# Attention of the second block: second score products two steps behind the first, exponentials ahead of the maxima's transfer

## The chip, the cores and the metric

One Trainium2 chip, one of its cores. The metric is the time of one execution in device microseconds (us), the median over several. The engines: TensorE (PE, matrix products), VectorE (DVE), ScalarE (ACT), GpSimd (POOL) and SyncE (SP), which only issues DMAs. ACT can issue DMAs from a queue of its own.

## What is computed

Two transformer blocks, one behind the other, on x of 8 × 512 × 256 (8 items, 512 tokens, 256 features; 16 heads of 16). Cut to what matters here, the second block:

```python
qkv = (x @ qkv_w).reshape(b, n, 3, H, D)
scores = jnp.einsum('bhnd,bhmd->bhnm', q, k) * scale
scores = jnp.where(mask, scores, -jnp.inf)      # mask: the keys of 384 to 511 that are padding
attn = jax.nn.softmax(scores, axis=-1)
out = jnp.einsum('bhnm,bhmd->bhnd', attn, v)
attn_out = out.transpose(0, 2, 1, 3).reshape(b, n, c) @ proj_w + proj_b
x = x + gate_msa[:, None, :] * _modulate(_layernorm(attn_out), shift_msa, scale_msa)
mlp_out = jax.nn.gelu(x @ fc1_w + fc1_b, approximate=False) @ fc2_w + fc2_b
x = x + gate_mlp[:, None, :] * _modulate(_layernorm(mlp_out), shift_mlp, scale_mlp)
```

The mask that the second block gets is the logical not of the valid positions, so only keys among the last 128 count. The kernel reads from the data that this is so and then takes a short form of the attention, with 128 keys a head; it has the general form beside it.

## The kernel before

The work goes item by item: turn n attends item n (n = 0 to 7 of the first block, n = 8 to 15 of the second) and carries along the dense work of the items beside it: for item n − 1 the turning of the attention rows ("t3"), the output product ("wout"), the turning for the MLP ("t2"), its first layer ("up") and second layer ("down"), and for item n + 1 the turning of the input ("t1") and its queries and keys ("qk"). The order on each engine is written out by hand. In the short form (`short(n)`, the second block) a turn is a loop over steps p; each step has three places k = 3p, 3p + 1, 3p + 2 at which the table `HEADS` names dense pieces, and `HEADS_DOWN` says which chunks of the second layer TensorE does there. There are 32 chunks, eight for each of the four token tiles: one product of 128 × 256 in f32, which stands as two rows in TensorE's order of the trace. The walks over `HEADS` are made by every engine, so a piece that is moved in the table moves on TensorE, ACT and VectorE alike.

Heads go in pairs q = 0 to 7. What happens to one pair:

- `pair_scores_of` (L919): four products give the scores of all 512 queries against 128 keys for both heads, in the two `score` banks. It waits for `peaks_ready` of the pair before, since that read the same bank.
- `peaks_of` on VectorE: the maximum over keys (L1432), split into a high and a low part (L1437, L1439).
- `turn_peaks` (L926): TensorE turns these into rows, in the first `score` bank.
- `take_peaks` on VectorE (L1447): the negated rows go into `peaks`, of which there is one. It waits for `peaks_loaded` of the pair before.
- `load_peaks` on ACT (L1131): a DMA on ACT's queue puts `peaks` (8 KB) into four rows of `q_rows`.
- `turned_scores_of` (L938): the second score products, keys on the partitions, with those four rows as further terms, so that the maximum is already subtracted. It waits for `peaks_loaded` of its pair and for the exponentials that free its `turned` bank.
- `head_exp` on ACT (L1125): the exponentials, two a pair.

For two pairs (four heads) there follow `attend_heads` (L948, value products), `take_heads_out` on ACT (L1145), `heads_to_tokens` (L956) and `divide_heads` on VectorE (L1455, L1457). The turn's t3 waits for the last of these.

Beside that SP loads for the next turn, in its own order: the stores of the queries and keys of item n + 1, the store of the output, the residual and modulation rows (L352, L355), then with `load_few(n + 1, g)` the query and key rows of the four groups g of four heads, each behind a `turned_ready` that says that group g's second score products of this turn are done.

ACT holds either the exponential's or the GELU's function table; `ACT_TABLE_LOAD` changes it.

Of the kernel before, what the change touches and what calls it, by code (L numbers as in the profile page):

```python
# [18 lines left out]
def build(nc, d, out):  # L19
    B, L, D = d["x"].shape  # L20
    H = d["L0_cond_torus_scale"].shape[0]
# [47 lines left out]

    HEADS = {0: [("v", 3), ("t3", 0), ("t3", 1)], 1: [("t1", 0), ("t1", 1)], 2: [("wout", 0), ("wout", 1)],
# [3 lines left out]
             19: [("down", 0)], 23: [("down", 1)], 28: [("down", 2)], 35: [("down", 3)]}  # L76
    HEAD_STEPS = H // 2 + 4
    HEADS_DOWN = {16: (0, 6), 19: (6, 10), 20: (10, 11), 22: (11, 14), 23: (14, 16), 25: (16, 20), 26: (20, 21),
                  28: (21, 24), 29: (24, 25), 31: (25, 28), 34: (28, 29), 35: (29, 32)}

    ANY = {0: [("v", 0), ("v", 1)], 1: [("t3", 0), ("t3", 1)], 2: [("v", 2), ("v", 3)], 3: [("t1", 0), ("t1", 1)],
           4: [("wout", 0)], 5: [("wout", 1)], 6: [("wout", 2)], 7: [("wout", 3)], 9: [("qk", 0)],
# [32 lines left out]
    PLACE = []  # L115
    for second in (HEADS, ANY):
        order = listed(FIRST, -1)
# [12 lines left out]
    with ExitStack() as ctx:  # L130
# [134 lines left out]
        def short(n):  # L265
            return n >= B and not chosen["any"]
# [506 lines left out]
        def _(pe):  # L773
# [215 lines left out]
            def turn(n):  # L989
                if short(n):  # L990
                    for p in range(HEAD_STEPS):
                        attended = p >= 5 and p % 2 == 1
                        if 2 <= p < 2 + H // 2:
                            pair_scores_of(n, p - 2)
                        for k in range(3 * p, 3 * p + 2):
                            for piece, m in pieces(HEADS, k, n):
                                dense(piece, m)
                            if k in HEADS_DOWN:
                                down_chunks(n - 1, *HEADS_DOWN[k])
                        if attended:  # L1000
                            attend_heads(n, (p - 5) // 2)
                        if 3 <= p < 3 + H // 2:
                            turned_scores_of(n, p - 3)
                        if 2 <= p < 2 + H // 2:
                            turn_peaks(n, p - 2)
                        for piece, m in pieces(HEADS, 3 * p + 2, n):
                            dense(piece, m)
                        if 3 * p + 2 in HEADS_DOWN:
                            down_chunks(n - 1, *HEADS_DOWN[3 * p + 2])
                        if attended:  # L1010
                            heads_to_tokens(n, (p - 5) // 2)
                    return
                table, down = (FIRST, FIRST_DOWN) if n < B else (ANY, ANY_DOWN)
                for k in range(STEPS):
                    if k < UNITS and not begun(n, k) and not (n < B and amid(n, k - 1)):
                        scores(n, k)
                    if n + 1 < B and k in AHEAD:
                        scores(n + 1, AHEAD[k])
                    if k >= ATTEND and (k - ATTEND) % 4 == 0 and (k - ATTEND) // 4 < GQ:
                        attend(n, (k - ATTEND) // 4)  # L1020
                    if TURN <= k < TURN + UNITS:
                        turn_unit(n, k - TURN)
                    if k >= TOKENS and (k - TOKENS) % 4 == 0:
                        to_tokens(n, (k - TOKENS) // 4)
                    for i, (piece, m) in enumerate(pieces(table, k, n)):
                        if n < B and amid(n, k) and i == 2:
                            scores(n, k + 1)
                        dense(piece, m)
                    if n > 0 and k in down:
                        down_chunks(n - 1, *down[k])  # L1030
                for gq in range(GQ):
                    if TOKENS + 4 * gq >= STEPS:
                        to_tokens(n, gq)
# [9 lines left out]
        def _(act):  # L1043
# [120 lines left out]
            def turn(n):  # L1164
                if short(n):
                    for p in range(HEAD_STEPS):
                        for k in range(3 * p, 3 * p + 2):
                            for piece, m in pieces(HEADS, k, n):
                                dense(piece, m)
                        if p == 0 and n - 2 >= B:  # L1170
                            normalize(n - 2)
                        if p >= 5 and p % 2 == 1:
                            take_heads_out(n, (p - 5) // 2)
                        if 2 <= p < 2 + H // 2:
                            load_peaks(n, p - 2)
                        if 3 <= p < 3 + H // 2:
                            for a in range(2):
                                head_exp(n, 2 * (p - 3) + a)
                        for piece, m in pieces(HEADS, 3 * p + 2, n):
                            dense(piece, m)  # L1180
                        if n == B and p == 6:
                            take_high(w_out, raw_out[1], "wout_loaded", "out_high", 2)
                        if n == B and p == HEAD_STEPS - 1:
                            take_high(w_up, raw_up[1], "wup_loaded", "up_high", 2)
                    return
                for k in range(STEPS):
                    if k >= OUT and (k - OUT) % 4 == 0:
                        take_out(n, (k - OUT) // 4)
                    for piece, m in pieces(FIRST if n < B else ANY, k, n):
                        dense(piece, m)  # L1190
                    if 1 <= k <= UNITS:
                        exps(n, k - 1)
                    if n < B and k + 2 < UNITS and bias_by_act(k + 2):
                        make_bias(n, k + 2)
                    if n == B - 1 and k in (6, 7):
                        take_qkv_high(k - 6)
                    if n == B and k == 15:
                        piece_ready(act, ("wout", TT - 1), n - 1)
                        take_high(w_out, raw_out[1], "wout_loaded", "out_high", 2)
                for gq in range(GQ):  # L1200
                    if OUT + 4 * gq >= STEPS:
                        take_out(n, gq)
                if n == B:
                    take_high(w_up, raw_up[1], "wup_loaded", "up_high", 2)
# [10 lines left out]
        def _(dve):  # L1215
# [293 lines left out]
            def turn(n):  # L1509
                if short(n):  # L1510
                    for p in range(HEAD_STEPS):
# [15 lines left out]
                            dense(piece, m)  # L1527
                        if p == 1 and n == B:
                            first_norm("stats", 1, n - 1)
                        if p >= 5 and p % 2 == 1:  # L1530
                            divide_heads(n, (p - 5) // 2)
                        if n == B and p == 6:
                            take_low(w_out, raw_out[1], "out_high", "out_split", 2)
                    if n == B:
# [84 lines left out]
```

## Time and profile before

| | |
|---|---|
| time, median of 3 runs | 1422.58 us (1421.8 to 1427.55) |
| the profiled execution: time, span | 1422.82 us, 1421.0 us |
| TensorE busy | 1298.0 us, 91% |
| VectorE, ACT, GpSimd busy | 798.7, 765.3, 755.1 us |
| mean granted TensorE clock | 0.982 |

In the rows below, a time at a row's start is in us from the start of the span, then comes the duration of the row (rows of equal instructions in a row are merged, with their count behind the x), and in brackets how long the engine sat idle before it and what it then waited for. "issue" in such a bracket means that the trace shows nothing that it waited for. Busy times of TensorE are modelled: products are pipelined, so the start of one to the start of the next is the better measure.

### The profile page before, as it was taken

The page shows a single profiled execution, that of the slowest core. Times are in us where ns is not written, and L with a number is a line of the kernel's source. Part 1 is how long each engine was busy: PE and PEld are TensorE (multiplying, and loading weights), DVE is VectorE, ACT ScalarE, POOL GpSimd, SP SyncE. Part 2 cuts the span into 40 slices and gives each one's busy share as a digit, 9 for nine tenths or more (in the row PEclk, how much of TensorE's full clock was granted, in tenths as well). Part 3 has the DMA queues.
Part 4 walks back from the last instruction along what each step waited for, and adds up shares of the span by engine and source line. Part 5 has one row for each costly group of instructions (what it writes and reads, how often), then busy time and mean ns, then how long its engine had stood idle before and what let it go on. Part 6 is the DMA issues. An engine that isn't in the chain of part 4 may idle for free. (4 is left out here: it accounts for less than half of the span.)

```text
span 1421.0 us, 24552 instructions
## 1 busy us (share of the span) xinstructions
PE 1298.0 (91%) x8789; PEld 994.6 (70%) x8789; DVE 798.7 (56%) x2240; ACT 765.3 (54%) x1262; POOL 755.1 (53%) x939
## 2 busy tenths in 40 slices
PE   4899999999999999999999996989888888888887
PEld 3577777777787788777787785666666666565656
DVE  3766746746646646647646544464564646464452
ACT  3466665765765765756755753454535444454432
POOL 3698867867877777777777751021322224041323
PEclk9899999999999999999999998999999999999988
DMA  8432322322323313213314316363425243332100
GB/s 259 138 117 56 87 86 53 98 75 67 99 60 84 94 49 90 91 44 91 100 36 111 112 25 185 99 181 87 163 58 163 78 138 101 114 130 74 46 2 30
DMA packets 98259, 133.98 MB, mean 94 GB/s; under 512 B 16802, under 2 KB 51498, under 8 KB 98130
## 3 DMA queue, kind: packets, MB, share of 16 engines
q1 hardware_dynamic: 96850, 131.80, 31.8%
q8 instruction: 73, 1.20, 0.4%
q10 hardware_dynamic: 1280, 0.53, 0.1%
q14 instruction: 56, 0.46, 0.1%
HBM read 72.64 MB, written 58.75 MB: 92 GB/s over the span
## 5 line engine op out<-in xcount | busy, mean ns | idle before, releaser
L1398 DVE CUSTOM_DVE_ANT_0 shifted<-score,bias 128x512 f32<-128x512 f32 x512 | 332.1, 686 | 259.8 <-PE score L869 138.3
L631 POOL TENSOR_SCALAR shifted<-shifted,row_max 128x512 f32<-128x512 f32 x512 | 359.6, 714 | 200.7 <-DVE row_max L1398 199.0
L1109 ACT ACTIVATE probs<-turned 128x512 f32<-128x512 f32 x512 | 277.7, 595 | 222.6 <-PE turned L881 222.0
L881 PE MATMUL turned<-ident,shifted 128*128 128x128 f32 x2048 | 270.2, 275 | 6.4 <-POOL shifted L631 6.0
L881 PEld LDWEIGHTS turned<-ident,shifted 128*128 128x128 f32 x2048 | 232.5, 141 | 59.6 <-issue 28.9
L797 PE MATMUL dense<-w_down,hidden 128*128 128x256 f32 x1024 | 255.0, 381 | 0.8 <-ACT hidden L1090 0.8
L624 POOL TENSOR_SCALAR bias<-dist,scale 128x1024 f32<-128x1024 f32 x192 | 217.2, 1132 | 14.0 <-DMA down_bias<-in_L_cond_b 14.0
L869 PE MATMUL score<-k_rows,q_rows 97*128 97x512 f32 x512 | 202.4, 457 | 13.7 <-DMA k_rows<-mask_neg 4.3
L797 PEld LDWEIGHTS dense<-w_down,hidden 128*128 128x128 f32 x1024 | 180.3, 190 | 31.0 <-issue 9.6
L777 PE MATMUL dense<-feat_m,w_up 128*128 128x512 f32 x768 | 191.1, 401 | 3.4 <-ACT hidden L1090 1.8
L777 PEld LDWEIGHTS dense<-feat_m,w_up 128*128 128x128 f32 x768 | 144.5, 192 | 37.3 <-ACT hidden L1090 5.2
L869 PEld LDWEIGHTS score<-k_rows,q_rows 97*128 97x128 f32 x512 | 92.6, 191 | 48.2 <-DVE row_max L1398 33.7
L896 PE MATMUL pv<-probs,v_ext 128*32 128x256 f32 x2048 | 123.8, 382 | 0.2 <-DVE attn L1423 0.2
L1125 ACT ACTIVATE probs<-turned 128x512 f32<-128x512 f32 x128 | 69.5, 595 | 96.4 <-DVE peaks L1447 90.6
L645 POOL CAST mask_colf<-mask_col 128x4 f32<-128x4 uint8 x8 | 1.5, 186 | 224.1 <-PE pv L948 216.4
L1090 ACT ACTIVATE hidden<-dense,up_bias 128x512 f32<-128x512 f32 x128 | 85.6, 688 | 57.8 <-PE dense L777 57.4
L777 PE MATMUL dense<-feat_a,w_qkv 128*128 128x512 f32 x384 | 104.9, 415 | 2.8 <-DVE feat_a L1352 2.8
L896 PEld LDWEIGHTS pv<-probs,v_ext 128*32 128x32 f32 x2048 | 60.2, 109 | 53.8 <-issue 16.8
L1432 DVE TENSOR_REDUCE row_max<-score 128x8 f32<-128x1024 f32 x64 | 78.1, 1221 | 27.7 <-PE score L919 27.7
L1447 DVE TENSOR_SCALAR peaks<-score 16x128 fp32r<-16x128 f32 x64 | 17.7, 276 | 117.7 <-PE score L926 117.6
L777 PEld LDWEIGHTS dense<-feat_a,w_qkv 128*128 128x128 f32 x384 | 71.0, 196 | 15.8 <-issue 3.2
L1077 ACT ACTIVATE qk_high<-dense 128x512 fp32r<-128x512 f32 x64 | 38.2, 597 | 68.3 <-PE dense L777 68.2
(138 smaller groups left out, 1546.4 us busy)
## 6 DMA issues: line engine op xcount, KB each, us to landing
qk_rows<-qk_high SPq DMA_DIRECT2D x128, 256.0 KB
q_rows<-qk_rows SPq DMA_DIRECT2D x64, 384.0 KB
qk_rows<-qk_low SPq DMA_DIRECT2D x64, 256.0 KB
k_rows<-qk_rows SPq DMA_DIRECT2D x68, 192.0 KB
x_in_t<-in_x SPq DMA_DIRECT2D x8, 512.0 KB, 4.8
x_res<-in_x SPq DMA_DIRECT2D x8, 512.0 KB, 5.7
x_mid<-x_norm SPq DMA_DIRECT2D x8, 512.0 KB, 3.2
x_in_t<-x_mid SPq DMA_DIRECT2D x8, 512.0 KB, 3.9
```

What stands on the lines that cost most here:

```text
L624: pool.tensor_scalar(bias[:, u % 2, :, :], dist[:, 2 * half:2 * half + 2, :], scale[:, h:h + 1], 0.0, ALU.mult, ALU.add).then_inc(s["bias_ ...
L631: ins = pool.tensor_scalar(shifted[:, u % 3, i, :], shifted[:, u % 3, i, :], -1.0, row_max[:, t % 6:t % 6 + 1], ALU.mult, ALU.add)
L777: mm = pe.matmul(out_ap, left, right, start=(i == 0), stop=(i == len(terms) - 1))
L797: mm = pe.matmul(bank_of(piece, m)[:, 0:D], hidden[:, c, P * i:P * i + P], w_down[:, c, :], start=(c == 0), stop=(c == FCH - 1))
L869: pe.matmul(score_bank[t % 2], q_rows[0:KROWS, g % 2, j // 2, q0:q0 + P], k_rows[0:KROWS, g % 2, j // 2, j % 2, :], start=True, stop=True) ...
L881: mm = pe.transpose(turned_bank[z % 2][:, HALF * kk + P * i:HALF * kk + P * i + P], shifted[:, u % 3, i, P * kt:P * kt + P], ident[:, :])
L896: mm = pe.matmul(pv_bank[SLOT * j:SLOT * j + SLOT, 0:HALF], v_ext[:, kt, HG * (gq // 2) + j, :], probs[:, (4 * gq + j) % RING, kt, :], sta ...
L1090: act.activation(hidden[:, i, :], bank[:, :], ACT.Gelu_apprx_tanh if m < B else ACT.Gelu, bias=up_bias[:, i:i + 1]).then_inc(used(piece, m ...
L1109: act.activation(probs[:, u % RING, 2 * pair:2 * pair + 2, :], turned_bank[z % 2][:, :].rearrange("p (a c) -> p a c", a=2), ACT.Exp)\
L1125: act.activation(head_probs[:, h % RING, :], turned_bank[h % 2][:, :], ACT.Exp)\
L1398: dve.tensor_tensor_reduce(shifted[:, u % 3, i, :], score_bank[t % 2], bias[:, u % 2, i, :], 1.0, 3.0e38, ALU.add, ALU.min, row_max[:, t % ...
L1432: dve.tensor_reduce(row_max[:, :].rearrange("p (a t) -> p t a", a=2), pair_scores, mybir.AxisListType.X, ALU.max).then_inc(s["peak_ready"], 1)
```

## The change

On the second block's short form only:

- A turn has 13 steps instead of 12. The second score products and the exponentials of pair q stand in step q + 4 instead of q + 3; attention of two pairs in steps 6, 8, 10, 12 instead of 5, 7, 9, 11.
- On ACT the exponentials of a step stand ahead of `load_peaks` of the step, not behind it.
- `turn_peaks` of pair 0 stands behind the last piece "qk" of step 2, not ahead of it.
- In `HEADS`, ("t1", 0) stands ahead of the two t3, and the last two "down" pieces (for ACT and VectorE: when the tile is taken over) stand at 29 and 38 instead of 28 and 35. `HEADS_DOWN` spreads the 32 chunks anew.

```diff
-    HEADS = {0: [("v", 3), ("t3", 0), ("t3", 1)], 1: [("t1", 0), ("t1", 1)], 2: [("wout", 0), ("wout", 1)],
+    HEADS = {0: [("v", 3), ("t1", 0), ("t3", 0), ("t3", 1)], 1: [("t1", 1)], 2: [("wout", 0), ("wout", 1)],
...
-             19: [("down", 0)], 23: [("down", 1)], 28: [("down", 2)], 35: [("down", 3)]}
-    HEAD_STEPS = H // 2 + 4
-    HEADS_DOWN = {16: (0, 6), 19: (6, 10), 20: (10, 11), 22: (11, 14), 23: (14, 16), 25: (16, 20), 26: (20, 21),
-                  28: (21, 24), 29: (24, 25), 31: (25, 28), 34: (28, 29), 35: (29, 32)}
+             19: [("down", 0)], 23: [("down", 1)], 29: [("down", 2)], 38: [("down", 3)]}
+    HEAD_STEPS = H // 2 + 5
+    HEADS_DOWN = {16: (0, 5), 17: (5, 6), 19: (6, 9), 20: (9, 10), 22: (10, 15), 23: (15, 16), 25: (16, 18), 26: (18, 19),
+                  28: (19, 23), 29: (23, 24), 31: (24, 26), 32: (26, 27), 35: (27, 30), 38: (30, 32)}
...
# TensorE, turn(n), short form
-                        attended = p >= 5 and p % 2 == 1
+                        attended = p >= 6 and p % 2 == 0
...
-                            attend_heads(n, (p - 5) // 2)
-                        if 3 <= p < 3 + H // 2:
-                            turned_scores_of(n, p - 3)
-                        if 2 <= p < 2 + H // 2:
+                            attend_heads(n, (p - 6) // 2)
+                        if 4 <= p < 4 + H // 2:
+                            turned_scores_of(n, p - 4)
+                        if 2 < p < 2 + H // 2:
                             turn_peaks(n, p - 2)
                         for piece, m in pieces(HEADS, 3 * p + 2, n):
                             dense(piece, m)
+                        if p == 2:
+
+                            turn_peaks(n, 0)
...
# ACT
-                        if p >= 5 and p % 2 == 1:
-                            take_heads_out(n, (p - 5) // 2)
+                        if p >= 6 and p % 2 == 0:
+                            take_heads_out(n, (p - 6) // 2)
+                        if 4 <= p < 4 + H // 2:
+                            for a in range(2):
+                                head_exp(n, 2 * (p - 4) + a)
                         if 2 <= p < 2 + H // 2:
                             load_peaks(n, p - 2)
-                        if 3 <= p < 3 + H // 2:
-                            for a in range(2):
-                                head_exp(n, 2 * (p - 3) + a)
```

The place of heads_to_tokens on TensorE and of divide_heads on VectorE moves with the attention in the same way.

How that moves instructions. TensorE at the start of a middle turn, from the turning of the attention rows on, before:

```order
L785 MATMUL dense<-ident,attn 128x128 x8
L785 MATMUL dense<-ident,x_in_t 128x128 x8
L777 MATMUL dense<-w_out,feat_m 128x256 x24
L777 MATMUL dense<-feat_a,w_qkv 128x512 x12
L919 MATMUL score<-k_rows,q_rows 128x256 x4
L777 MATMUL dense<-feat_a,w_qkv 128x512 x6
L849 MATMUL dense<-ident,shifted 128x128 x8
L926 MATMUL score<-ident,split_peak 16x128
L777 MATMUL dense<-feat_a,w_qkv 128x512 x6
L919 MATMUL score<-k_rows,q_rows 128x256 x4
```

and now:

```order
L785 MATMUL dense<-ident,x_in_t 128x128 x4
L785 MATMUL dense<-ident,attn 128x128 x8
L785 MATMUL dense<-ident,x_in_t 128x128 x4
L777 MATMUL dense<-w_out,feat_m 128x256 x24
L777 MATMUL dense<-feat_a,w_qkv 128x512 x12
L919 MATMUL score<-k_rows,q_rows 128x256 x4
L777 MATMUL dense<-feat_a,w_qkv 128x512 x6
L849 MATMUL dense<-ident,shifted 128x128 x8
L777 MATMUL dense<-feat_a,w_qkv 128x512 x6
L926 MATMUL score<-ident,split_peak 16x128
L919 MATMUL score<-k_rows,q_rows 128x256 x4
```

Half of the input's turning has gone ahead of the attention rows, and the turning of the first maxima has changed places with a qk product.

TensorE from the scores of pair 3 to those of pair 5 (steps 5 to 7), before:

```order
L919 MATMUL score<-k_rows,q_rows 128x256 x4
L797 MATMUL dense<-w_down,hidden 128x256 x6
L948 MATMUL pv<-probs,v_ext 32x512 x4
L938 MATMUL turned<-q_rows,k_rows 128x512 x2
L926 MATMUL score<-ident,split_peak 16x128
L956 MATMUL pv<-ident,head_out 128x128 x4
L919 MATMUL score<-k_rows,q_rows 128x256 x4
L797 MATMUL dense<-w_down,hidden 128x256 x4
L938 MATMUL turned<-q_rows,k_rows 128x512 x2
L926 MATMUL score<-ident,split_peak 16x128
L797 MATMUL dense<-w_down,hidden 128x256
L919 MATMUL score<-k_rows,q_rows 128x256 x4
```

and now:

```order
L919 MATMUL score<-k_rows,q_rows 128x256 x4
L797 MATMUL dense<-w_down,hidden 128x256 x5
L938 MATMUL turned<-q_rows,k_rows 128x512 x2
L926 MATMUL score<-ident,split_peak 16x128
L797 MATMUL dense<-w_down,hidden 128x256
L919 MATMUL score<-k_rows,q_rows 128x256 x4
L797 MATMUL dense<-w_down,hidden 128x256 x3
L948 MATMUL pv<-probs,v_ext 32x512 x4
L938 MATMUL turned<-q_rows,k_rows 128x512 x2
L926 MATMUL score<-ident,split_peak 16x128
L797 MATMUL dense<-w_down,hidden 128x256
L956 MATMUL pv<-ident,head_out 128x128 x4
```

The second score products (L938) here belong to pairs 2 and 3 before, and to pairs 1 and 2 now; the value products have moved one step on.

ACT from the first GELUs of a middle turn, before:

```order
L1090 ACT_TABLE_LOAD
L1090 ACTIVATE hidden<-dense,up_bias 128x512 x4
L1131 DMA q_rows<-peaks 4x4x128
L1125 ACT_TABLE_LOAD
L1125 ACTIVATE probs<-turned 128x512 x2
L1090 ACT_TABLE_LOAD
L1090 ACTIVATE hidden<-dense,up_bias 128x512 x4
L1131 DMA q_rows<-peaks 4x4x128
L1125 ACT_TABLE_LOAD
L1125 ACTIVATE probs<-turned 128x512 x2
L1145 ACTIVATE head_out<-pv 128x512
```

and now (the lines of the changed file are three further on):

```order
L1093 ACT_TABLE_LOAD
L1093 ACTIVATE hidden<-dense,up_bias 128x512 x4
L1134 DMA q_rows<-peaks 4x4x128
L1093 ACTIVATE hidden<-dense,up_bias 128x512 x4
L1128 ACT_TABLE_LOAD
L1128 ACTIVATE probs<-turned 128x512 x2
L1134 DMA q_rows<-peaks 4x4x128
L1128 ACTIVATE probs<-turned 128x512 x2
L1134 DMA q_rows<-peaks 4x4x128
L1148 ACTIVATE head_out<-pv 128x512
```

The eight GELUs stand together, two table loads are gone, and each DMA of the maxima stands behind the exponentials of its step.

## Rows read from the trace of the kernel before

**Rows 1.** Page, sections 1 and 2: busy us of each engine; granted clock by slices.

```profile
PE 1298.0 (91%) x8789; PEld 994.6 (70%) x8789; DVE 798.7 (56%) x2240; ACT 765.3 (54%) x1262; POOL 755.1 (53%) x939
...
PEclk9899999999999999999999998999999999999988
```

**Rows 2.** TensorE in order of time: first row of the first short turn, and behind the eighth.

```profile
861.41 1.23 PE L777 MATMUL dense<-w_qkv,feat_a 128*128 128x256 f32 x6 [4.34 <-issue]
...
1372.23 1.10 PE L785 MATMUL dense<-ident,attn 128*128 128x128 f32 x8 [1.62 <-DVE attn L1457]
```

**Rows 3.** TensorE's waits, 861 to 1372: us in total, times, longest us.

```profile
PE turned L938 <- issue: 14.7, 17, 2.5
...
PE score L926 <- DVE split_peak L1439: 10.0, 8, 1.4
...
PE score L919 <- DVE peaks L1447: 8.1, 19, 1.0
...
PE dense L785 <- DVE attn L1457: 6.0, 7, 0.9
...
PE pv L948 <- ACT probs L1125: 5.0, 8, 0.9
...
PE dense L777 <- ACT hidden L1090: 1.8, 8, 0.2
```

**Rows 4.** TensorE in order of time, the turn from 1060 to 1117.

```profile
1069.12 0.28 PE L926 MATMUL score<-ident,split_peak 128*16 128x128 f32 x1 [1.38 <-DVE split_peak L1439]
...
1070.63 0.64 PE L919 MATMUL score<-k_rows,q_rows 97*128 97x256 f32 x4
...
1084.38 0.62 PE L938 MATMUL turned<-q_rows,k_rows 101*128 101x512 f32 x2
...
1085.49 0.74 PE L919 MATMUL score<-k_rows,q_rows 97*128 97x256 f32 x4 [0.37 <-DVE peaks L1447]
...
1086.06 2.76 PE L797 MATMUL dense<-w_down,hidden 128*128 128x256 f32 x12
...
1091.39 0.71 PE L938 MATMUL turned<-q_rows,k_rows 101*128 101x512 f32 x2 [1.51 <-issue]
...
1104.93 0.28 PE L926 MATMUL score<-ident,split_peak 128*16 128x128 f32 x1
...
1113.97 1.07 PE L948 MATMUL pv<-probs,v_ext 128*32 128x512 f32 x8 [0.88 <-ACT probs L1125]
```

**Rows 5.** VectorE in order of time, the same turn and the start of the next.

```profile
1068.98 1.28 DVE L1355 TENSOR_TENSOR feat_m<-dense,feat_m 128x512 fp32r<-128x512 f32 x2
...
1070.18 0.27 DVE L1447 TENSOR_SCALAR peaks<-score 16x128 fp32r<-16x128 f32 x1
...
1104.70 0.17 DVE L1439 TENSOR_TENSOR split_peak<-row_max,split_peak 128x8 fp32r<-128x8 f32 x1
...
1119.91 1.29 DVE L1355 TENSOR_TENSOR feat_m<-dense,feat_m 128x512 fp32r<-128x512 f32 x2 [1.38 <-ACT feat_m L1072]
```

**Rows 6.** Stretch 1156 to 1160: us, busy us (instructions) by engine, clock, DMA share, GB/s.

```profile
1156.00:1160.00 4.00, 4.00 (x18) 3.39 (x18) 2.22 (x5) 1.08 (x2) 0.00 (x0) 0.64 0.01 2
```

**Rows 7.** ACT, TensorE and SP in order of time, and the stretch from 1214 to 1221.

```profile
1110.05 0.64 ACTq L1131 DMA_DIRECT2D q_rows<-peaks  x1
...
1111.95 0.70 PE L938 MATMUL turned<-q_rows,k_rows 101*128 101x512 f32 x2
...
1213.90 0.33 SPq L382 DMA_DIRECT2D q_rows<-qk_rows  x1
...
1214.27 0.64 ACTq L1131 DMA_DIRECT2D q_rows<-peaks  x1
...
1221.18 0.71 PE L938 MATMUL turned<-q_rows,k_rows 101*128 101x512 f32 x2 [2.49 <-issue]
...
1214.00:1221.00 7.00, 4.40 (x24) 2.86 (x24) 1.80 (x4) 3.04 (x5) 0.00 (x0) 1.00 0.76 207
```

**Rows 8.** Page, section 5: busy us, mean ns of one | idle before, releaser.

```profile
L1432 DVE TENSOR_REDUCE row_max<-score 128x8 f32<-128x1024 f32 x64 | 78.1, 1221 | 27.7 <-PE score L919 27.7
```

More of the change, by code:

```diff
@@ L1010, in turn @@
                         if attended:
-                            heads_to_tokens(n, (p - 5) // 2)
+                            heads_to_tokens(n, (p - 6) // 2)
                     return
@@ L1529, in turn @@
                             first_norm("stats", 1, n - 1)
-                        if p >= 5 and p % 2 == 1:
-                            divide_heads(n, (p - 5) // 2)
+                        if p >= 6 and p % 2 == 0:
+                            divide_heads(n, (p - 6) // 2)
                         if n == B and p == 6:
```

## The prediction

> **What bounds the kernel now.** I read the page first: TensorE is busy 91% of the 1421.0 us span, the other engines 53 to 56%, and its granted clock is near full speed nearly everywhere [rows 1]. So the question is what TensorE waits for in the stretch that is changed. The short turns of the second block lie between the two rows of [rows 2]: 1372.2 − 861.4 = 510.8 us for eight turns, 63.9 us each. The list of TensorE's waits over that stretch [rows 3] holds 14.7 us before the second score products (L938), put down to "issue", 10.0 before the turning of the peaks (L926), 8.1 before the first score products (L919), 6.0 before the turning of the attention rows, 5.0 before the value products (L948) and 1.8 inside the up products. These, 45.6 us, are what the change can touch.
>
> What "issue" hides: a second score product needs its heads' negated maxima in `q_rows`, which ACT's queue puts there by a DMA (`load_peaks`, L1131), and a DMA's landing is no instruction of the trace. In an undisturbed step the DMA is issued at 1110.05 and the product runs at 1111.95: it lands within 1.9 us [rows 7]. In a disturbed one it is issued at 1214.27, just behind SP's load of the next turn's query rows at 1213.90, and the product starts only at 1221.18, 6.9 us later, in a stretch in which the DMAs moved 207 GB/s [rows 7]. **Of queues** the row says: a DMA of 8 KB waited for the large ones beside it. The Trainium skill, "DMA: Bandwidth & Descriptors", section "Queues, rings and completion order", says two things: an engine goes round robin between the rings at packet granularity, by which this DMA would land in about the undisturbed time, and the semaphore's write lands only after all earlier writes of that DMA engine, across its queues. The trace agrees with the second: 6.9 us against 1.9.
>
> **The change part by part.** A *chunk* below is one product of `down_chunks`; six take 2.76 us, so 0.46 each [rows 4]. All counts are for eight turns.
>
> 1. `HEADS` puts the first turning of the next input (t1, 0) ahead of the turning of the attention rows (t3). TensorE waits there 0.9 us for the divided rows in any case; what sets the pace afterwards is VectorE, idle 1.38 us before its first low half at 1119.91 and then without a gap until it has written the maxima [rows 5]. One low half (half of 1.29 us) moves into that idle time; the first output product itself starts only some 0.2 us earlier, and VectorE must wait for its end, so I take 0.45 us of the 0.65. Seven turns have a t1: **−3.2 us**.
>
> 2. `turn_peaks(n, 0)` goes behind the last qk product (1.5 us of work). The 1.38 us wait at 1069.12 [rows 4] goes, but not the time: the next thing on TensorE is now the score product of pair 1, which needs `take_peaks(0)`, and VectorE does that only behind two low halves of t2, at 1070.18 + 0.27 = 1070.45 [rows 5]. Before, the product started at 1070.63 [rows 4]. So 0.1 us in each of six turns and about 1.0 in the first, where TensorE ran that qk product at half clock behind the wait: **−1.6 us**. What is late next is VectorE's two low halves.
>
> 3. The exponentials of pair 0 leave step 3. ACT then does all eight GELUs in a row and loads two function tables in a turn instead of four; the wait inside the up products goes [rows 3]: **−1.8 us**. The rest of ACT's saving is beside other work.
>
> 4. The second score products follow two steps behind: the waits at their old place go, **−14.7 us** [rows 3].
>
> 5. The last value product has three chunks (1.4 us) before it instead of one, against exponentials that let the value products start 2.0 us behind the second score product (1111.95 [rows 7] to 1113.97 [rows 4]): of 5.0 us [rows 3] 0.5 stays, **−4.5 us**.
>
> 6. In one or two steps of a turn the turning of the peaks waits without a mark in the list: 1104.93, right behind VectorE's split, which starts at 1104.70 and takes 0.17 [rows 4, 5]; product and chunks before it end 0.37 us earlier. Five chunks stand there now instead of four: eight times 0.37, **−3.0 us**.
>
> 7. Added: step 5 has no value products and no turning back. Its turning of the peaks is followed by a wait of 0.46 instead of 0.37 (**+0.7 us**), and steps 6 and 8 have one chunk where 0.65 us are needed (0.1 each: **+1.6 us**).
>
> 8. Added: `peaks` is one buffer. `take_peaks(q)` waits on VectorE until the DMA of pair q−1 has landed, and the scores of pair q+1 wait for `take_peaks(q)`, with VectorE's next reduction behind them. This wait never told before, because TensorE had already waited for that landing. Now the landing of pair 2 is needed by the scores of pair 4. I count from the end of the up products, U: second products 0.47, turning 0.11, wait 0.46, scores 0.57, five chunks 2.30, second products 0.54, turning 0.11, chunk 0.46: TensorE is there at U + 5.0. U comes 0.7 us earlier than the row 1084.38 [rows 4] (0.21 of step 3, 0.5 of the product that left): 1083.7, and U + 5.0 is 1088.7. The old landing is the start of the waiting product, 1091.39 [rows 4]. SP's load of the next turn's rows (by the code 96 × 2 × 512 × 4 bytes = 393 KB and two of 49 KB, 0.5 MB) now starts 4 us later, behind `turned_ready`; by the 207 GB/s [rows 7] the traffic before the landing is 2.4 us shorter. So landing 1088.9, `take_peaks` and its way 0.4: 1089.3, a wait of 0.6. In the turn of 1221.18 the same gives 1.6. Four turns had over 1 us there: four times 1.1, **+4.4 us**. The landings of pairs 3, 5 and 7 meet SP's loads of one group each, land some 4 us behind their issue and are needed 4.5 us on: 0.1 a turn, **+0.8 us**.
>
> Sum: −3.2 − 1.6 − 1.8 − 14.7 − 4.5 − 3.0 + 0.7 + 1.6 + 4.4 + 0.8 = −21.3 us. The profiled execution took 1422.8 us (span 1421.0), the median of three is 1422.6: **1401.5 us**, 2.7 us less in each turn.
>
> By the round-robin rule of the page alone, term 8 would be nothing and the time 1396; by rows it is 5 us.
>
> Unknown both ways is the **clock**. At full clock nearly throughout, the trace shows 0.64 in 1156 to 1160, a mixture of its two levels, 1.2 and 2.4 GHz, right behind a wait of over 2 us [rows 6]; that costs (1 − 0.64) × 4 = 1.4 us. The second block has about four such places. With shorter waits one or two can go, with waits in a new place one or two can come: 0 taken, ±3 us as bounds.
>
> **The rivals.**
> - *The small DMA no longer waits at all*, since it is issued ahead of the load it used to follow. For: the issue at 1214.27 stood behind the one at 1213.90. Against: the store of the output and the two loads ahead of it stay. Term 8 gone: 1396 us.
> - *The wait only changes its place.* If the landing keeps its old time (the backlog alone sets it), the scores of pair 4 wait 1091.4 + 0.4 − 1088.7 = 3.1 us in the turn of 1091.39, over 4 in that of 1221.18, and about 15 us in all instead of 4.4: 1412 us. For: the six DMAs ahead of it; against: 2.4 us of traffic do leave.
> - *Slower: a turn is a chain of steps, and a step more costs its own length.* If a step is carried by scores, reduction, split, turning and `take_peaks`, not by TensorE's work, the thirteenth step costs 4.2 us (8 × 4.2 = 33.6), minus what is saved: 1422.8 + 33.6 − 21.3 = 1435 us. It decides where TensorE's own work in a step falls under the loop: scores 0.57, reduction 1.22 [rows 8], two copies of 0.17, turning 0.27, `take_peaks` 0.27, 2.7 us and with the signals between engines about 3.3. Against: only 19 of 64 steps show a wait before L919, 8.1 us in all, 0.4 each [rows 3].
> - *No net change*: the second products of the last pairs and the value products fall together at the turn's end, and ACT, with head output, exponentials of pair 6 and of pair 7 in a row, holds both up by 2 us a turn: 8 × 2 − 21.3, about 1417 us. Against: ACT is busy 54% of the span [rows 1].
>
> **How the numbers follow.** Forecast 0.62, no wait 0.12, wait displaced 0.16, no change 0.06, slower 0.04. A measurement tells about 0.5% (7 us) from no change. The first three lie below 1415.5: faster 0.90, same 0.06, slower 0.04. The range takes in no DMA wait and 3 us of clock below (1396 − 3) and the displaced wait and 3 us of clock above (1412 + 3): 1393 to 1415.
>
> **What the new profile would show.** Right: turns of 61 us; no wait of TensorE before L926 at a turn's start but one of 1.1 to 1.2 before the scores of pair 1; next to no "issue" before the second products; two table loads a turn; waits before the scores of pair 4 put down to VectorE's `peaks`, 0.5 to 1.7 us in the middle turns. Wrong: waits of 3 us there, half clock behind them, or steps that last 4 us with idle TensorE in all of them.

## The result, and the profile after

The changed kernel takes 1401.95 us (median of 4, 1399.86 to 1405.66) against 1422.44 us beside it: 20.5 us less, a ratio of 0.984 (95% interval 0.982 to 0.987). Forecast were 1401.5 us. Run again later it took 1399.24 us (median of 5), ratio 0.984 (0.982 to 0.986). One of the twelve executions of an experiment below (ACT's order alone, in the kernel before) took 7096 us and counts in no ratio.

The page of the changed kernel, in answer to [rows 1]; the span of this execution is 1403.9 us:

```profile
PE 1294.1 (92%) x8789; PEld 994.4 (71%) x8789; DVE 803.9 (57%) x2240; ACT 744.4 (53%) x1246; POOL 757.0 (54%) x939
...
PEclk9899999999999999999999998999999999999998
```

TensorE's first row of the short turns and the one behind the eighth, in answer to [rows 2]:

```profile
862.61 1.65 PE L777 MATMUL dense<-w_qkv,feat_a 128*128 128x256 f32 x6 [4.62 <-issue]
```

```profile
1356.74 1.09 PE L785 MATMUL dense<-ident,attn 128*128 128x128 f32 x8 [1.62 <-DVE attn L1460]
```

That is 494.1 us for eight turns instead of 510.8, so 16.7 of the 17.1 us by which the two spans differ. The profiled execution took 1405.66 us.

What TensorE waits for over the eight turns (us in total, times, longest), in answer to [rows 3]:

```profile
PE score L919 <- DVE peaks L1450: 23.8, 29, 3.8
PE dense L777 <- DVE feat_m L1358: 9.2, 8, 1.8
...
PE dense L785 <- DVE attn L1460: 3.3, 6, 0.9
...
PE dense L785 <- DVE feat_a L1358: 2.1, 1, 2.1
PE turned L938 <- issue: 1.7, 5, 0.5
PE score L926 <- DVE split_peak L1442: 0.7, 1, 0.7
```

Of [rows 3], the 14.7 us before the second products are 1.7, the waits before the value products and inside the up products have gone from the list, and 10.0 before L926 are 0.7. Two lines have grown: 8.1 before the first score products are 23.8, now with a longest of 3.8 us, and the output products (L777 from `feat_m`) wait 9.2, 1.2 us in a middle turn. Against that stand 1.8 us at the output products and 5.6 at the input's turning (L785) that the kernel before waited for the same `feat_m`: most of this wait has only moved. The 2.1 us for `feat_a` are one wait, in the second turn, before the second half of the input's turning. At the same piece the kernel before waits 1.36 us. Together with 0.68 us before the output products and a granted clock of 0.70 from 932 to 936 it makes the start of this turn, up to the scores of pair 1, 19.6 us long instead of 17.7. The prediction has no term for that.

```profile
932.87 0.63 PE L785 MATMUL dense<-ident,x_in_t 128*128 128x128 f32 x4 [2.13 <-DVE feat_a L1358]
```

The start of one turn on TensorE, in order of time:

```profile
1114.18 1.09 PE L785 MATMUL dense<-ident,attn 128*128 128x128 f32 x8 [0.47 <-DVE attn L1460]
...
1117.05 2.98 PE L777 MATMUL dense<-w_out,feat_m 128*128 128x256 f32 x24 [1.21 <-DVE feat_m L1358]
...
1129.40 0.73 PE L919 MATMUL score<-k_rows,q_rows 97*128 97x256 f32 x4 [1.11 <-DVE peaks L1450]
```

The wait before the turning of the attention rows is 0.47 instead of 0.9, the wait before L926 is gone, and there is the foretold one of 1.11 before the scores of pair 1.

Steps 4 and 5 of the same turn, where the largest wait stands: TensorE, then VectorE, then the DMA issues of ACT and of SP.

```profile
1143.38 0.75 PE L919 MATMUL score<-k_rows,q_rows 97*128 97x256 f32 x4 [0.37 <-DVE peaks L1450]
1143.97 2.32 PE L797 MATMUL dense<-w_down,hidden 128*128 128x256 f32 x10
...
1151.08 0.71 PE L919 MATMUL score<-k_rows,q_rows 97*128 97x256 f32 x4 [3.78 <-DVE peaks L1450]
```

```profile
1145.63 0.17 DVE L1442 TENSOR_TENSOR split_peak<-row_max,split_peak 128x8 fp32r<-128x8 f32 x1
1150.65 0.28 DVE L1450 TENSOR_SCALAR peaks<-score 16x128 fp32r<-16x128 f32 x1 [4.86 <-DMA q_rows<-peaks]
```

```profile
1143.36 0.64 ACTq L1134 DMA_DIRECT2D q_rows<-peaks  x1
...
1150.97 0.64 ACTq L1134 DMA_DIRECT2D q_rows<-peaks  x1
```

```profile
1139.70 0.94 SPq L433 DMA_DIRECT2D out<-x_norm  x1
1140.68 0.51 SPq L352 DMA_DIRECT2D shifted<-x_mid  x1
1141.24 1.46 SPq L355 DMA_DIRECT2D shifted<-mod_rows  x1
1146.85 0.34 SPq L382 DMA_DIRECT2D q_rows<-qk_rows  x1
```

The maxima of pair 2 leave ACT's queue at 1143.36 and land only at 1150.65, 7.3 us later, where `take_peaks` of pair 3 stops waiting for "DMA q_rows<-peaks". In front of them lie the output store and the loads of the residual and modulation rows, 0.5 MB each. The scores of pair 4 wait 3.78 us for that. By the trace the last of these loads, issued at 1141.24, lands 9.1 us later, at 1150.3, 0.3 us before `take_peaks`. In the five turns with such a wait the time from the maxima's issue to `take_peaks` is 4.8, 5.4, 7.3, 4.9 and 4.3 us; in the first four it ends 0.2 to 0.3 us behind the landing of the modulation rows, in the fifth 1.0 us before it. This is the wait of `peaks`, the single buffer, that the prediction's eighth term names; in five turns it is 1.24, 1.89, 3.78, 1.39 and 0.79 us, 9.1 in all, and what stands behind two of them has a price of its own (stretches, with columns as in [rows 6]):

```profile
1152.00:1156.00 4.00, 4.00 (x16) 1.56 (x15) 2.18 (x5) 0.16 (x1) 0.00 (x0) 0.57 0.01 2
```

A granted clock of 0.57 of full speed for four microseconds right behind the wait of 3.78: mostly at 1.2 GHz. Behind the wait of 1.89 it is 0.65 from 1086 to 1090. From the scores of pair 4 to those of pair 5 TensorE takes 4.40 us in six turns and 6.04 in the turns with the waits of 1.89 and 3.78, so the clock takes another 3.3 us.

### The profile page after: what moved, and what is told of

Same layout as the page of the kernel before. It is cut to its first block, busy times and chain, and to the rows that moved or that the text cites. A ratio compares the mean times of both kernels' runs of the same rounds, so it can differ in the third digit from the quotient of the medians.

```text
span 1403.9 us, 24536 instructions
## 1 busy us (share of the span) xinstructions
PE 1294.1 (92%) x8789; PEld 994.4 (71%) x8789; DVE 803.9 (57%) x2240; ACT 744.4 (53%) x1246; POOL 757.0 (54%) x939
## 4 chain that ended last, share of the span: by engine, by line
PE 68%; DVE 19%; issue 4%; DMA 3%; ACT 3%; POOL 2%; SPq 1%; DVEq 0%; POOLq 0%; ACTq 0%
PE dense L777 17%; PE dense L797 15%; PE turned L881 11%; PE pv L896 7%; DVE shifted L1401 6%; PE score L869 6%; DVE x_norm L1241 3%; PE turned L938 2%; PE score L919 2%; PE pv L948 2%; DMA q_rows<-peaks 2%; DVE feat_m L1358 2%; PE dense L785 1%; POOL shifted L631 1%; ACT probs L1112 1%
## 5 line engine op out<-in xcount | busy, mean ns | idle before, releaser
L797 PE MATMUL dense<-w_down,hidden 128*128 128x256 f32 x1024 | 258.2, 383 | 0.8 <-ACT hidden L1093 0.8
L777 PE MATMUL dense<-feat_m,w_up 128*128 128x512 f32 x768 | 188.3, 399 | 1.6 <-DVE feat_m L1358 1.6
L777 PEld LDWEIGHTS dense<-feat_m,w_up 128*128 128x128 f32 x768 | 144.6, 191 | 32.4 <-issue 2.0
L777 PE MATMUL dense<-feat_a,w_qkv 128*128 128x512 f32 x384 | 103.5, 410 | 2.8 <-DVE feat_a L1355 2.8
L777 PEld LDWEIGHTS dense<-feat_a,w_qkv 128*128 128x128 f32 x384 | 70.2, 194 | 16.1 <-issue 3.2
L1101 ACT ACTIVATE bias<-dist,scale 128x1024 f32<-128x1024 f32 x64 | 73.7, 1151 | 0.0
```

The costliest lines, as they stand in the source:

```text
L777: mm = pe.matmul(out_ap, left, right, start=(i == 0), stop=(i == len(terms) - 1))
L797: mm = pe.matmul(bank_of(piece, m)[:, 0:D], hidden[:, c, P * i:P * i + P], w_down[:, c, :], start=(c == 0), stop=(c == FCH - 1))
L1101: act.activation(bias[:, u % 2, :, :], dist[:, 2 * half:2 * half + 2, :], ACT.Copy, scale=scale[:, h:h + 1]).then_inc(s["act_bias_ready"], 1)
```

## The experiments

All times are medians, ratios against runs of the kernel before on the same chip at the same time.

**Two buffers for the maxima.** The changed kernel with

```diff
-        peaks = sb("peaks", [4 * TT, P], F32R)
+        peaks = sb("peaks", [4 * TT, 2, P], F32R)
...
-                if count > 0:
-                    dve.wait_ge(s["peaks_loaded"], 16 * count)
-                dve.tensor_scalar(peaks[:, :], score_bank[0][0:4 * TT, 0:P], -1.0, None, ALU.mult)\
+                if count > 1:
+                    dve.wait_ge(s[f"peaks_loaded{q % 2}"], 16 * (count // 2))
+                dve.tensor_scalar(peaks[:, q % 2, :], score_bank[0][0:4 * TT, 0:P], -1.0, None, ALU.mult)\
```

and the semaphore split in two in the DMA and before the second products.

> The changed kernel with two peaks buffers, each with a semaphore of its own, so that VectorE waits for the landing of the pair before last. Theory 'one buffer': the waits before the scores of pair 4 (1.24, 1.89, 3.78, 1.39 and 0.79 us in five turns, 9.1 in all) go, at most 0.5 us a turn comes back before the second score products, and the time falls by 7 to 9 us against the changed kernel's 1402, to 1393 to 1395. Theory 'late landing': the DMA lands later than two steps in any case, the 9 us come back as 'issue' before L938, and the time stays at 1399 to 1402.

Measured: 1391.55 us, ratio 0.979 (0.977 to 0.981). TensorE's waits:

```profile
PE score L919 <- DVE peaks L1450: 15.2, 24, 1.1
...
PE turned L938 <- issue: 1.4, 4, 0.5
```

The longest wait before the first scores is 1.1 again, which is the one of pair 1, and the second products wait 1.4 us instead of 1.7: nothing came back there. From the scores of pair 3 to those of pair 4 every turn takes 3.94 or 3.95 us, from there to pair 5 4.40 or 4.41, so the half clock has gone with the waits. One buffer is what kept the DMA's landing on TensorE's way. The gain is 10.4 us against the changed kernel's 1401.95 and 7.7 against its later 1399.24; expected were 7 to 9. The waits and the clock of the changed kernel's trace add up to 12.4, those of its later trace to 5.1.

**t1 back behind t3.** The changed kernel with the old first entries of `HEADS`:

```diff
-    HEADS = {0: [("v", 3), ("t1", 0), ("t3", 0), ("t3", 1)], 1: [("t1", 1)], 2: [("wout", 0), ("wout", 1)],
+    HEADS = {0: [("v", 3), ("t3", 0), ("t3", 1)], 1: [("t1", 0), ("t1", 1)], 2: [("wout", 0), ("wout", 1)],
```

> The changed kernel with both t1 behind t3 again in HEADS. Theory 'VectorE sets the pace at the turn's start': 0.45 us more in each of seven turns, 3.2 us, 1405; the wait before t3 is 0.9 again and the one before the output products falls from 1.2. Rival 'TensorE's own waits only change places there': no difference, 1402.

Measured: 1400.03 us, ratio 0.983 (0.981 to 0.985), the same as with the change. In the trace a middle turn takes 17.3 us from its first product to the scores of pair 1, against 17.1: 0.2 us a turn, less than half of what I had, and under what the runs can tell. In the second turn it is the other way round, 19.2 us here against 19.6 with t1 ahead, which has the wait of 2.13 us shown above.

**The turning of pair 0's maxima back in its place.**

```diff
-                        if 2 < p < 2 + H // 2:
+                        if 2 <= p < 2 + H // 2:
                             turn_peaks(n, p - 2)
...
-                        if p == 2:
-
-                            turn_peaks(n, 0)
```

> The changed kernel with the turning of pair 0's maxima ahead of the last qk product again. My theory: the wait of 1.38 before L926 comes back and the one of 1.1 before the scores of pair 1 goes; 0.1 us a turn and about 1 us in the first, 1402.5 to 1403.6 and not to be told from the changed kernel. Rival 'the wait was worth its size': 8 times 1.1 to 1.4, 1411.

Measured: 1402.58 us, ratio 0.986 (0.983 to 0.988). Its waits:

```profile
PE score L919 <- DVE peaks L1447: 12.5, 19, 2.6
...
PE score L926 <- DVE split_peak L1439: 9.9, 8, 1.4
```

9.9 us before L926 instead of 0.7, 12.5 instead of 23.8 before L919 (4.3 of these are smaller waits before the scores of pair 4, 4.8 us against 9.1), and no time moved that the medians can tell. The rival's 1411 did not come. What TensorE waits for in this place is VectorE, and the wait mostly changes its name. The trace shows one thing more:

```profile
1069.76 0.38 PE L926 MATMUL score<-ident,split_peak 128*16 128x128 f32 x1 [1.38 <-DVE split_peak L1439]
1069.79 2.91 PE L777 MATMUL dense<-feat_a,w_qkv 128*128 128x512 f32 x6
```

The six rows behind the wait take 2.91 us instead of some 1.6; the granted clock from 1070 to 1072 is 0.50. This happens in four of the six turns with a wait of 1.38, and there the stretch from the scores of pair 0 to those of pair 2 is 1.4 to 1.7 us longer than in the changed kernel, 6.1 us in all; the waits of 1.11 before the scores of pair 1 in the changed kernel have full clock behind them. This profiled execution, 1408.11 us, was the slowest of six, so the medians hold less of it. What the edit is worth is therefore open between nothing and some 3 us.

**ACT's order back.** The changed kernel with `load_peaks` ahead of the exponentials:

```diff
+                        if 2 <= p < 2 + H // 2:
+                            load_peaks(n, p - 2)
                         if 4 <= p < 4 + H // 2:
                             for a in range(2):
                                 head_exp(n, 2 * (p - 4) + a)
-                        if 2 <= p < 2 + H // 2:
-                            load_peaks(n, p - 2)
```

> The changed kernel with load_peaks ahead of the exponentials on ACT again, everything else as changed. My theory: with the products two steps behind, the exponentials' order on ACT is beside TensorE's work; 0 to 1 us, 1402 to 1403. Rival 'it is the exponentials' order that brings the gain': ACT waits up to 4 us for the maxima with the exponentials behind it, TensorE waits before the value products and the second scores, 1406 to 1410.

Measured: 1413.23 us, ratio 0.993 (0.991 to 0.996): 11.3 us slower than the changed kernel. My theory fell. The rival named the right place, the value products, but 1406 to 1410 us was too little, and no new wait stands before the second products. TensorE's waits, and a late step of one turn on TensorE and on ACT:

```profile
PE pv L948 <- ACT probs L1128: 9.3, 16, 1.0
```

```profile
1227.45 0.82 PE L938 MATMUL turned<-q_rows,k_rows 101*128 101x512 f32 x2
...
1230.63 1.06 PE L948 MATMUL pv<-probs,v_ext 128*32 128x512 f32 x8 [0.95 <-ACT probs L1128]
```

```profile
1228.73 0.64 ACTq L1134 DMA_DIRECT2D q_rows<-peaks  x1
1229.49 1.09 ACT L1128 ACTIVATE probs<-turned 128x512 f32<-128x512 f32 x2 [2.64 <-DVE peaks L1450]
```

The same step with the exponentials first (the changed kernel, ACT):

```profile
1227.85 1.09 ACT L1128 ACTIVATE probs<-turned 128x512 f32<-128x512 f32 x2 [2.30 <-PE turned L938]
1228.42 0.64 ACTq L1134 DMA_DIRECT2D q_rows<-peaks  x1
```

The second product of the pair starts at 1227.45 here and, in the changed kernel, at 1227.14. Its exponentials follow 2.04 us behind it where the DMA comes first (ACT waits for VectorE's `peaks`, then spends 0.64 us on issuing), and 0.71 us where it comes second. With two or three chunks in front of the value products that difference is not covered: 0.21 and 0.95 us in each of eight turns, 9.3 in all.

**The lag alone.** The three edits above taken back together; left are the lag of two steps, the thirteenth step and the new spread.

> The changed kernel with t1, the turning of pair 0's maxima and ACT's order all back as before: what is left is the lag of two steps with the new spread of the chunks. By the single runs so far (t1 worth nothing or 1 to 2 us, the turning nothing, ACT's order 11 us): 1413 to 1415, so still 8 us under the kernel before. Rival 'the pieces only work together': 1420 or more.

Measured: 1412.34 us, ratio 0.993 (0.991 to 0.994). Its waits:

```profile
PE score L926 <- DVE split_peak L1439: 10.5, 9, 1.4
PE score L919 <- DVE peaks L1447: 10.2, 20, 1.2
PE pv L948 <- ACT probs L1125: 9.3, 16, 0.9
```

The lag takes the 14.7 us before the second products away, and half of the gain is eaten by value products that wait for their exponentials. So the lag and the spread are worth 10 us, ACT's order another 11 on top, and the two edits at the turn's start nothing that can be told.

**ACT's order alone, in the kernel before.**

```diff
-                        if 2 <= p < 2 + H // 2:
-                            load_peaks(n, p - 2)
                         if 3 <= p < 3 + H // 2:
                             for a in range(2):
                                 head_exp(n, 2 * (p - 3) + a)
+                        if 2 <= p < 2 + H // 2:
+                            load_peaks(n, p - 2)
```

> The kernel before with nothing but the exponentials ahead of load_peaks on ACT. Theory 'order pays only with the lag': there the second products still wait for the same landing, the value products have a whole step behind their exponentials and the last ones have no load_peaks beside them; 1420 to 1423. Rival 'the order pays by itself': 1411 to 1413, as much as it was worth in the changed kernel.

Measured: 1426.95 us, ratio 1.0025 (1.0008 to 1.0042): nothing gained, if anything a little lost, and 4 us above what I had expected.

```profile
PE turned L938 <- issue: 16.9, 18, 2.4
...
PE pv L948 <- ACT probs L1125: 5.0, 8, 0.9
```

The value products wait 5.0 us as before and the second products 16.9 instead of 14.7. The order on ACT pays with the lag only.

**Group 0's load later.** The changed kernel with

```diff
-                    sp.wait_ge(s["turned_ready"], TILES * (m - 1) + TILES // G * (g + 1))
+                    sp.wait_ge(s["turned_ready"], TILES * (m - 1) + TILES // G * (2 if g == 0 else g + 1))
```

> The changed kernel with SP's load of the next turn's group 0 held until the second products of group 1 instead of group 0 (two steps later). Theory 'a DMA waits for what is issued behind it, too': pair 2's maxima land earlier, the waits before the scores of pair 4 (9.1 us) fall under 4, some come back one or two steps later where two loads now follow one another; 1396 to 1401. Rival 'only the backlog ahead of it counts': the same 9 us at the same place, 1402.

Measured: 1398.54 us, ratio 0.983 (0.980 to 0.985). From the scores of pair 3 to those of pair 4, 3.95 us where nothing waits, it takes 5.54, 5.06, 5.41, 4.98 and 4.63 us in the five turns: waits of 5.9 us in all. The time is in my range, but the waits lie between my two theories, and the second trace of the unchanged changed kernel (below) has 5.1 us there. The run tells nothing sure about group 0's load as a cause; what it shows is that waits of 0.7 to 1.6 us remain when that load is issued 13 us behind the DMA (1153.33 against 1140.06 in one turn).

**The residual and modulation loads later.** The changed kernel, in SP's turn:

```diff
-                load_res(n)
-                load_mod(n)
                 if n + 1 < N:
                     load_few(n + 1, 0)
+                load_res(n)
+                load_mod(n)
+                if n + 1 < N:
                     load_few(n + 1, 1)
```

> The changed kernel with the loads of the residual and of the modulation rows (0.5 MB each) issued behind group 0's load, one step later. Theory 'the backlog ahead of it counts': pair 2's maxima land within 3 us of their issue and the wait before the scores of pair 4 goes, but those of pair 5 or 6 wait instead, 2 to 5 us each turn, because 1.5 MB now lie in front of their landing; 1402 to 1415. Rival 'only group 0's load counts': no difference at pair 4.

Measured: 1393.30 us, ratio 0.979 (0.977 to 0.981). SP and ACT issues in one turn (this file has its lines one further on), and TensorE's waits:

```profile
1139.94 0.34 SPq L382 DMA_DIRECT2D q_rows<-qk_rows  x1
...
1141.99 0.44 SPq L352 DMA_DIRECT2D shifted<-x_mid  x1
1142.48 0.50 SPq L355 DMA_DIRECT2D shifted<-mod_rows  x1
```

```profile
1140.31 0.64 ACTq L1135 DMA_DIRECT2D q_rows<-peaks  x1
...
1144.55 0.64 ACTq L1135 DMA_DIRECT2D q_rows<-peaks  x1
```

```profile
PE score L920 <- DVE peaks L1451: 14.8, 24, 1.1
...
PE turned L939 <- issue: 1.6, 5, 0.5
```

The two loads now stand 1.7 and 2.2 us behind the DMA of pair 2's maxima (1140.31), not in front, and the wait before the scores of pair 4 is gone in every turn (3.94 or 3.95 us). Group 0's load stands 0.4 us in front of it and does no harm. The waits that I expected at pairs 5 and 6 did not come: those steps take 4.40 or 4.41 and 3.91 to 3.93 us in all middle turns. VectorE alone still waits for landings, 8.7 us over the eight turns against 23.6 with the change as it is, and the scores of pair 7 come at most 0.2 us later for it. One of these landings, issued at 1148.63 behind a group's load of 1148.27:

```profile
1148.63 0.64 ACTq L1135 DMA_DIRECT2D q_rows<-peaks  x1
```

```profile
1152.29 0.28 DVE L1451 TENSOR_SCALAR peaks<-score 16x128 fp32r<-16x128 f32 x1 [1.12 <-DMA q_rows<-peaks]
```

That is 3.7 us from issue to landing behind 0.5 MB, against 4.3 to 7.3 behind 1.5 MB.

**Both together.**

> The changed kernel with two peaks buffers and with the residual and modulation loads behind group 0's load. Theory 'both take away the same wait': no more than either alone, 1390 to 1394, the middle turns 58.6 us as with either. Rival 'each takes a part': 1382 to 1386.

Measured: 1391.96 us, ratio 0.978 (0.977 to 0.980), middle turns of 58.5 to 58.7 us. Two buffers and the later loads take away the same wait; 1391.5 to 1393.3 us is what either reaches. Both beat the changed kernel.

**The later loads in the kernel before.** The same edit of SP's order and nothing else.

> The kernel before with only SP's loads of the residual and modulation rows behind group 0's load. Theory 'the backlog ahead of the small DMA sets its landing': the waits before the second products of pair 2 (7.5 of the 14.7 us) go, unless they come back one pair later; 1413 to 1418. Rival 'group 0's load alone, which stays right beside it, sets it': 1421 to 1424.

Measured: 1413.94 us, ratio 0.994 (0.992 to 0.995).

```profile
PE turned L939 <- issue: 5.3, 11, 1.6
PE pv L949 <- ACT probs L1126: 5.0, 8, 0.9
```

14.7 us before the second products are 5.3, with none before those of pair 2. The 9.0 us against 1422.95 are about two fifths of what the change brings on this chip (23.7 us); they could be had by moving two lines.

**The changed kernel again.**

> The changed kernel itself once more, on the chip of these three, to know how far its time repeats: 1400 to 1404.

Measured: 1399.24 us, ratio 0.984 (0.982 to 0.986).

```profile
PE score L919 <- DVE peaks L1450: 20.0, 29, 1.3
...
PE turned L938 <- issue: 1.9, 5, 0.6
```

In this execution the waits before the scores of pair 4 come to 5.1 us (0.84, 1.00, 1.25, 1.07 and 0.94 over the 3.95 us), none is followed by half clock, and the span is 1396.4 us, 7.5 less than in the other. The landing of that DMA accounts for 7.3 us between the two executions, 4.0 of waits and 3.3 of clock. They differ elsewhere too, by 1.8 us before the first scores and by small amounts the other way in the turns, which nearly cancel. The median lies 0.8 us under what I had expected.

## Why the prediction was right, and where it was not

The time was forecast within 0.5 us of the median, and faster; that it came so near is in part luck, as the steps show. By its own steps:

1. *t1 ahead of t3, −3.2 us.* Too large. The wait before t3 is shorter as said, but the output products wait 1.21 us for the low halves, and each of the five middle turns gains 0.2 us up to the scores of pair 1, 1.0 us in all. The second turn loses 0.4 us, and the first differs by more from trace to trace than the edit could do. What the prediction missed is that VectorE, which it rightly took for the one that sets the pace, is waited for at the output products, too.
2. *The turning behind the last qk product, −1.6 us.* Right in kind and place: 1.11 us before the scores of pair 1, to be put down to VectorE. The medians cannot tell it from nothing. The half clock behind the old wait, which the term counts in the first turn only, stood in four more turns of the trace with this edit taken back.
3. and 4. *−1.8 and −14.7 us.* Right: no wait inside the up products, 1.7 us left before the second products.
5. *−4.5 us.* Right in its number, wrong in what it rests on. It counts on value products that can start 2.0 us behind the second score product, which the changed kernel has only because ACT's order was changed as well: with the old order they start 3.2 us behind it (1227.45 to 1230.63). With the old order the lag would have put 9.3 us of waits before the value products. The prediction gave that edit no price of its own, though "behind what is it queued on ACT" was the question to ask: the DMA waits for VectorE, takes 0.64 us to issue, and the exponentials stand behind both.
6. and 7. *−3.0, +0.7 and +1.6 us.* Not separable in a trace. Together the steps do better than said. Compare turns with hardly a DMA wait, from the scores of pair 1 to the next turn: 43.8 to 44.2 us in the old kernel with the later loads, 41.4 to 41.6 in the changed one with two buffers and the later loads. That is some 2.5 us a turn, where my terms 3, 5, 6 and 7 give 0.88 and what is left of "issue" in that kernel another 0.66. Where the remaining microsecond comes from is open; I have not tried it.
8. *The single buffer, +4.4 us.* The mechanism, its place and the engine were right, and two buffers remove it. The size was 9.1 us and 3.3 us of half clock in one execution and 5.1 us without any in another. The working took group 0's load to be what shortens the backlog. The loads that matter are the residual and modulation rows in front of the DMA: with these behind it the wait goes, with group 0's load still 0.4 us ahead of it.

So the sum came out right with errors against each other: the eighth term too small by 1 to 8 us and the first too large by more than 2, against steps that save about 1 us a turn more than I counted. The sum of −21.3 us also stands between the two pairs of executions that it could be held against: the spans of the first differ by 17.1 us, and the later trace is 24.6 us under the trace of before. The rival "the wait only changes its place" had 3.1 us in one turn, over 4 in another and about 15 in all: there were 3.78 at most and 9.1 in all. What the prediction named as a sign of being wrong, a wait of 3 us with half clock behind it, did appear in one turn of the first trace and in none of the second. The rival "the small DMA no longer waits" was 1396; without that wait the kernel takes 1392. The rival "a step more costs its own length" did not come: a middle turn takes 60 us where no landing is very late, and 58.6 where none is late, against 61.5 in the old kernel with the later loads.

The small DMA lands 4.3 to 7.3 us behind its issue with 1.5 MB in front of it, 3.7 with 0.5 MB and within 1.9 with none [rows 7]. Of the two rules that the prediction took from the Trainium skill ("DMA: Bandwidth & Descriptors", "Queues, rings and completion order") the trace again agrees with the one on completions, by which the semaphore's write comes behind earlier writes on other queues of the same DMA engine, and not with a landing that round robin alone would give: four of the five late landings come 0.2 to 0.3 us behind that of the last large load. The traces show landings only, not the order of work inside a DMA engine, so the mechanism itself is argued and not shown; that it is the loads in front that matter is shown by moving them.

## What to carry to other kernels

When a consumer is moved further behind a transfer, look for what else waits for the same landing: a single staging buffer turns "needed two steps later" into "its successor is needed one step later". An issue queue is an engine's order too: a DMA that must wait for another engine, put ahead of work that is ready, holds that work, and the cheapest place for large transfers is behind the small one that somebody waits for.

## What was not expected of the hardware

A DMA of 8 KB took 4.3 to 7.3 us from issue to landing behind three of 0.5 MB, and its landing varied enough to put 7.3 us between two executions of one kernel (1403.9 and 1396.4 us of span), of which 4.0 are waits and 3.3 the clock behind them. Waits of TensorE of 1.89 and 3.78 us were each followed by a stretch at about half clock that cost 1.64 us (6.04 us against 4.40 for the same work), while waits of 1.24 and 1.39 in the same trace were not. In the run with the turning back in its place, four waits of 1.38 us were followed by half clock and two of the same length were not, so the length of the wait alone does not tell. Issuing one DMA keeps ACT's sequencer 0.64 us, and the exponentials behind it start only after that.
